# A new order of the work up to the third tile, and low weight parts made in PSUM, in a gated attention and FP4 feed-forward layer

## What is computed

```python
x = x + tanh(g_xattn) * attention(q=layernorm(x), k=v=ctx)        # x 8*512*512, ctx 8*77*512, one head of 512
x = x + tanh(g_ffn) * ffn(layernorm(x))
# attention: softmax((q Wq' + bq)(ctx Wk')' / sqrt(512)) (ctx Wv' + bv) Wo' + bo
# ffn: fp4(silu(fp4(x) fp4(w_gate)') * (fp4(x) fp4(w_up)')) fp4(w_down)'    w_gate, w_up 1408*512, w_down 512*1408
# fp4(x): in blocks of 16 of the last axis, scale = max|x| / 6, x / scale rounded to 0, .5, 1, 1.5, 2, 3, 4, 6, times scale
```

## Time and profile before

| | us |
|---|---|
| median of 3 runs | 951.17 |
| profiled execution, its own time | 951.4 |
| its span on the core | 949.6 |
| TensorE matmul busy | 882.2 (93%) |
| VectorE busy | 760.6 (80%) |
| ScalarE busy | 294.1 (31%) |
| GpSimd busy | 336.9 (35%) |

### The profile page before, as it was taken

One profiled execution on the slowest core, in us unless ns is written; L12 is line 12 of the kernel. 1 busy time (PEld: TensorE's weight loads), 2 busy tenths in 40 slices (PEclk: granted clock), 3 DMA queues, 4 the chain that ended last, 5 costly groups with the idle time before them and its releaser, 6 DMA issues.

```text
span 949.6 us, 11466 instructions
## 1 busy us (share of the span) xinstructions
PE 882.2 (93%) x4233; PEld 457.6 (48%) x4233; DVE 760.6 (80%) x1235; ACT 294.1 (31%) x456; POOL 336.9 (35%) x279
## 2 busy tenths in 40 slices
PE   7959767887599999999999999999999999999996
PEld 4736323543245544554455445545554455444442
DVE  2799977989998879887988798879887988787842
ACT  1444321352223422342234223422342234223220
POOL 1266434424433333333333333333333333333330
PEclk9989878899889999999999999999999999999999
DMA  9512010000533432232223222322222333233222
GB/s 316 213 61 100 14 44 14 12 11 12 131 83 53 98 53 53 53 98 53 53 53 97 53 53 53 98 53 53 54 54 52 53 56 55 51 75 71 53 43 64
DMA packets 141450, 64.62 MB, mean 68 GB/s; under 512 B 126458, under 2 KB 126466, under 8 KB 141393
## 3 DMA queue, kind: packets, MB, share of 16 engines
q1 hardware_dynamic: 141393, 63.88, 28.4%
HBM read 22.76 MB, written 8.39 MB: 33 GB/s over the span
## 4 chain that ended last, share of the span: by engine, by line
PE 73%; DVE 15%; issue 5%; POOL 2%; DMA 2%; SPq 1%; ACT 1%; POOLq 0%; DVEq 0%
PE bank L1226 45%; PE bank L1292 23%; PE bank L1268 3%; DVE arena L844 3%; DVE arena L846 2%; PE bank L1220 2%; DVE wgu_lo L855 1%; POOL arena L428 1%; DMA arena<-in_L_ffn_w_up_dram 1%; DVE xn L905 1%; DVE xwork L801 1%; DMA x_T<-x_parts 1%; DVE h_parts L801 1%; DVE xwork L806 1%; DVE wd L887 0%
## 5 line engine op out<-in xcount | busy, mean ns | idle before, releaser
L1226 PE MATMUL bank<-wgu_hi,x_T 128*128 128x512 f16 (+1 forms) x1536 | 446.2, 365 | 18.1 <-DMA x_T<-x_parts 18.1
L1226 PE MATMUL bank<-wgu_lo,x_T 128*128 128x512 f16 (+1 forms) x768 | 280.4, 365 | 0.0
L1292 PE MATMUL bank<-wd,arena 128*128 128x512 f16 x1056 | 242.4, 387 | 16.9 <-DVE ring L1011 11.5
L1226 PEld LDWEIGHTS bank<-wgu_hi,x_T 128*128 128x128 f16 x1536 | 151.4, 99 | 178.5 <-issue 29.9
L1292 PEld LDWEIGHTS bank<-wd,arena 128*128 128x128 f16 x1056 | 104.7, 100 | 146.4 <-issue 21.7
L428 POOL TENSOR_TENSOR arena<-arena,h_r 128x1024 f32<-128x1024 f32 (+1 forms) x60 | 95.0, 1583 | 139.4 <-DVE h_r L808 139.4
L428 POOL TENSOR_TENSOR arena<-arena,h_s 128x1024 f32<-128x1024 f32 x64 | 89.3, 1395 | 135.0 <-DVE arena L846 135.0
L634 ACT ACTIVATE arena<-bank,scal 128x512 f32<-128x512 f32 (+1 forms) x96 | 62.3, 650 | 193.5 <-PE bank L1226 193.5
L1226 PEld LDWEIGHTS bank<-wgu_lo,x_T 128*128 128x128 f16 x768 | 75.7, 99 | 80.4 <-issue 7.8
L428 POOL TENSOR_TENSOR xwork<-xwork,x_s 128x512 f32<-128x512 f32 x32 | 33.9, 1059 | 185.7 <-DVE xwork L846 185.7
L987 DVE SCALAR_TENSOR_TENSOR arena<-arena,scal,bank 128x512 f32<-128x512 f32 (+1 forms) x90 | 63.0, 700 | 39.9 <-PE bank L1226 39.9
(11 more groups left out here) (117 smaller groups left out, 924.0 us busy)
## 6 DMA issues: line engine op xcount, KB each, us to landing
ring<-in_x_dram SPq DMA_DIRECT2D x8, 1024.0 KB, 5.5
out_dram<-ring SPq DMA_DIRECT2D x32, 256.0 KB, 2.0
arena<-in_L_ffn_w_down_dram SPq DMA_DIRECT2D x4, 704.0 KB, 4.1
arena<-in_L_ffn_w_gate_dram SPq DMA_DIRECT2D x5, 512.0 KB, 11.2
arena<-in_L_ffn_w_up_dram SPq DMA_DIRECT2D x5, 512.0 KB, 11.8
ring<-in_L_xattn_Wk_dram SPq DMA_DIRECT2D x4, 256.0 KB, 4.9
ring<-in_L_xattn_Wq_dram SPq DMA_DIRECT2D x4, 256.0 KB, 5.2
wd<-in_ctx_dram SPq DMA_DIRECT2D x1, 1024.0 KB, 8.8
```

What stands on the lines that cost most here:

```text
L1226: ended = e.matmul(at, l, r, start=(i == 0), stop=(i == len(terms) - 1))
L1292: ended = e.matmul(down_ps[:, :], l, r, start=(k == 0 and i == 0), stop=(k == KH - 1 and i == 2))
```

## The change

Four things, and new lists for all engines up to tile 3 (from `x_stats(4)` on they are as before, but for `h_low(0, 0)` and `h_low(0, 1)`, which now stand ahead of it).

1. The low parts: `gu_fold` multiplies the block scales by the inverse power on ScalarE, so that `gu_times` gives final values; `gu_high` is a plain copy; TensorE adds minus the high part to the bank (one f16 matmul with a negated identity); a ScalarE copy writes the low part. `gu_low` and `down_low` leave VectorE. `gu_times` now waits for the power.
2. The maximum over partitions: transpose of the column of maxima, a reduction on one partition, and a matmul with a row of ones.
3. The keys in two halves (`divmod(i, 5)`): five products before the first scores, five and four value products inside the loop over weight chunks; batch 0's values need `value_product(0)` alone and are read where `value_rows` puts them.
4. Three bf16 buffers for `gu_squares`; loads of weight chunks 0 to 3 between those of `Wk`, `Wq`; `x_turn(0)` ahead of all value moves.

```diff
-            i = WIDE_FROM + j % 2
-            return valo[:, i, :].bitcast(BF16)
+            at = x_parts[:, :] if j % 3 == 0 else x_T[j % 3 - 1][:, :, :].rearrange("p k n -> p (k n)")
...
-        mm = [("bqk", 0)] + [("key", i) for i in range(2 * KD + 2)] + [("vo", m) for m in range(KD)] + [("bvwo", 0)]
-        mm += [("val", r) for r in range(CT)]
+        mm = [("bqk", 0)] + [("key", i) for i in range(KEYS_HALF)] + [("vo", m) for m in range(KD)] + [("bvwo", 0), ("val", 0)]
+        mm += [("key", i) for i in range(KEYS_HALF, 2 * KEYS_HALF)] + [("val", r) for r in range(1, CT)]
         mm_bank = {name: n % 2 for n, name in enumerate(mm)}
-        mm_bank["val", CT - 1] = 5
...
# SyncE
+            for r in range(KD):
+                e.dma_start(stage_a[:, r, :], Wk[r * P:(r + 1) * P, :]).then_inc(loads[f"wk{r}"], 16)
+                e.dma_start(stage_b[:, r, :], Wq[r * P:(r + 1) * P, :]).then_inc(loads[f"wq{r}"], 16)
+                load_gu(r)
...
+            x_turn(0)
+            for n in range(1, NBATCH):
+                move_values(n)
# GpSimd
+            for j in range(EARLY):
+                gu_divide(j)
+            ln1(0)
+            gu_divide(5)
+            gu_times(0)
+            gu_divide(6)
+            gu_times(1)
+            gu_times(2)
+            gu_times(3)
+            gu_divide(7)
...
# ScalarE
-                if j >= 2:
-                    w.wait_ge(gu_neg, j - 1)
+                if j >= 3:
+                    w.wait_ge(gu_neg, j - 2)
...
+            def gu_low(n):
+                w.wait_ge(gu_less, n + 1)
+                e.copy(wgu_lo[:, :, gu_cols(n)], by_k(bank[gu_bank(n)][:, 0:D], KD)).then_inc(gu_lo, 1)
...
+            gu_folds(5, 7)
+            gu_squares(6)
+            for j in range(NPAIR):
...
+                gu_high(2 * j)
+                gu_high(2 * j + 1)
+                if j < 4:
+                    xn_copy(0, j)
+                    vo_copy(j)
...
+                gu_low(2 * j)
+                gu_low(2 * j + 1)
...
+            x_high(0)
+            x_squares(1)
+            x_high(1)
+            down_squares(0)
+            down_squares(1)
+            gate_silu(0, 0)
...
+            gate_silu(1, 2)
+            down_low(1)
+            x_high(3)
+            attention_part(1, "d soft")
+            attention_part(2, "a1")
# VectorE
+            value_rows(2)
+            value_rows(3)
+            x_low(0)
+            x_scales_of(1)
+            x_divide()
+            value_rows(4)
+            down_tops(0)
+            x_round(1)
+            down_tops(1)
+            down_tops(2)
+            x_low(1)
+            down_tops(3)
+            down_top_of()
+            down_scales(0)
+            x_stats(2)
+            power_of(d_top_turned, "d_top", pow_d, d_pow)
+            down_scales(1)
+            hidden(0, 0)
+            down_power()
+            down_scales(2)
+            hidden(0, 1)
+            x_scales_of(2)
+            ln1_stats(1)
+            x_divide()
+            down_round(0)
+            down_scales(3)
+            hidden(0, 2)
+            x_round(2)
+            ln1_apply(1)
...
+            x_low(3)
+            h_scales(0, 0)
+            h_scales(0, 1)
+            hidden(1, 2)
+            softmax(1)
# TensorE
+            def gu_subtract(n):
+                w.wait_ge(negated, 1)
+                w.wait_ge(gu_hi, n + 1)
+                e.matmul(by_k(bank[gu_bank(n)][:, 0:D], KD), neg_ident[:, :], wgu_hi[:, :, gu_cols(n)],
+                         start=False, stop=True, skip_group_check=True).then_inc(gu_less, 1)
...
+            key_product(0)
+            key_product(1)
+            top_turn("gu_top", top_gu, gu_top, gu_top_turned, gu_pow)
+            key_product(2)
+            power_spread("gu_pow", pow_gu, gu_pow, gu_pow_mm, p_ready)
+            key_product(3)
+            key_product(4)
...
+            for j in range(NPAIR):
+                if j == 6:
+                    prob_turn(0)
+                gu_turn(2 * j)
+                gu_turn(2 * j + 1)
+                if 1 <= j < 5:
+                    att_scores(0, j - 1)
+                if j < 4:
+                    att_turn(0, j)
+                    vo_product(j)
...
+                if j == 9:
+                    key_product(9)
+                    value_product(1)
+                if j == 10:
+                    value_product(2)
+                    value_product(3)
+                gu_subtract(2 * j)
+                gu_subtract(2 * j + 1)
+            value_product(4)
+            gate_up(0, 0, 0)
+            top_turn("d_top", top_d, d_top, d_top_turned, d_pow)
+            gate_up(0, 0, 1)
...
+            gate_up(0, 2, 1)
+            attention_part(0, "a3")
+            attention_part(0, "a4")
+            gate_up(1, 0, 0)
...
+            gate_up(1, 2, 0)
+            gate_up(1, 2, 1)
+            down_subtract(1)
+            attention_part(2, "a1")
+            gate_up(2, 0, 0)
```

More of the change, by code:

```diff
@@ new lines, in scalar_program @@
+            w.wait_ge(bqk_mm, 1)
+            e.copy(bqk_col[:, :], bank[mm_bank["bqk", 0]][:, 0:KD]).then_inc(bqk_sb, 1)
+            for r in range(CT):
+                rows = rows_of(r)
+                w.wait_ge(ctx_turned, r + 1)
+                e.copy(ctx_T[:, :, r * P:r * P + rows], by_k(bank[turn_bank["ctx", r]][:, 0:KD * rows], KD)).then_inc(ctx_sb, 1)
+            gu_squares(4)
+            w.wait_ge(loads["ga"], 16)
+            e.activation(tanh_a, tanh_a, ACT.Tanh).then_inc(tanh_done, 1)
@@ new lines, in scalar_program @@
+            w.wait_ge(loads["gf"], 16)
+            e.activation(tanh_f, tanh_f, ACT.Tanh).then_inc(tanh_done, 1)
+            key_copy(0)
+            key_copy(1)
+            key_copy(2)
+            gu_folds(0, EARLY)
+            key_copy(3)
+            gu_squares(5)
+            key_copy(4)
+            for r in range(KD):
+                w.wait_ge(wo_turned, r + 1)
+                e.copy(wo_T[:, :, r * P:(r + 1) * P], by_k(bank[turn_bank["wo", r]][:, 0:D], KD)).then_inc(wo_sb, 1)
+            gu_folds(5, 7)
@@ L757, in scalar_program @@
+            down_low(2)
+            down_high(3)
+            h_squares(0, 1)
+            gate_silu(2, 2)
+            down_low(3)
             h_high(0, 0)
@@ new lines, in vector_program @@
+            gu_tops(1)
+            gu_scales(1)
+            gu_tops(2)
+            gu_scales(2)
+            gu_round(0)
+            gu_tops(3)
+            gu_scales(3)
+            gu_round(1)
+            gu_tops(4)
+            gu_scales(4)
+            gu_tops(5)
+            ln1_stats(0)
+            for j in range(6, NPAIR):
+                gu_tops(j)
+            gu_top_of()
+            gu_scales(5)
+            power_of(gu_top_turned, "gu_top", pow_gu, gu_pow)
+            gu_scales(6)
@@ new lines, in vector_program @@
+            gu_power()
+            ln1_apply(0)
+            gu_round(2)
+            gu_round(3)
+            gu_scales(7)
+            gu_round(4)
+            gu_scales(8)
+            gu_round(5)
+            gu_scales(9)
+            gu_round(6)
+            scale_bo()
+            gu_scales(10)
+            gu_round(7)
+            softmax(0)
+            gu_round(8)
+            sums(0)
+            value_row()
+            value_rows(0)
+            gu_round(9)
+            for i in range(TILES):
+                values(0, i)
@@ new lines, in vector_program @@
+            x_stats(0)
+            gu_round(10)
+            x_scales_of(0)
+            x_divide()
+            value_rows(1)
+            x_round(0)
+            x_stats(1)
+            value_rows(2)
[11 more added lines that the diff above has]
+            down_top_of()
@@ new lines, in vector_program @@
+            x_stats(3)
+            down_round(2)
+            hidden(1, 0)
+            x_scales_of(3)
+            x_divide()
+            down_round(3)
+            hidden(1, 1)
+            x_round(3)
+            x_low(3)
[3 more added lines that the diff above has]
+            softmax(1)
+            sums(1)
+            hidden(2, 0)
+            values(1, 0)
+            h_round(0, 0)
+            hidden(2, 1)
+            values(1, 1)
+            h_round(0, 1)
@@ L1141, in vector_program @@
+            hidden(2, 2)
+            values(1, 2)
+            h_low(0, 0)
+            h_low(0, 1)
             attention_part(3, "a1")
@@ new lines, in tensor_program @@
+            key_product(1)
[4 more added lines that the diff above has]
+            key_product(4)
+            for r in range(KD):
+                take(turn_bank["wo", r], (wo_sb, r + 1))
+                w.wait_ge(loads["wo"], 16)
+                turn(turn_bank["wo", r], [stage_b[:, r, k * P:(k + 1) * P] for k in range(KD)]).then_inc(wo_turned, 1)
@@ new lines, in tensor_program @@
+            for j in range(NPAIR):
+                if j == 6:
+                    prob_turn(0)
[6 more added lines that the diff above has]
+                    vo_product(j)
+                if j == 4:
```

(16 more changed lines are left out.)

638 lines of the change are left out of this document (268 added, 370 removed).

## The result

The changed kernel takes 958.84 us (median of five, 956.52 to 959.73), the one before 951.17 (five runs by now, with the same median); the ratio is 1.0075, 95% interval 1.0052 to 1.0098: slower by 0.75%. 949.5 had been predicted, as no change; what came is the size of the first rival, 960.

A forecast was written before the change was run, and what follows sets the result against it. From tile 4 TensorE never idles, so the time hangs on tile 4's start, and that on when VectorE reaches x_stats(4). 951.4 + 0.4 (x_stats(4) later) - 2.3 (up to tile 4) = 949.5 us; own range 943 to 957.

The forecast's parts named there:

- the first rival: TensorE's two halts in tiles 0 to 2 are longer, x_stats(4) comes at 240: 960 us; chance 0.25.
- The bound: From tile 4 on TensorE never idles; the time is tile 4's start (271.7) plus 677.9 plus 1.8 us.
- Part 1: Setup, the power: scalars ready at 43.0 instead of 46.1, -3; shows only if the next list is short.
- Part 2: Setup, low parts: the 14.5 us removed from VectorE lie in POOL's shadow, worth nothing by themselves.
- Part 3: TensorE's list in the setup: 72.2 us plus waits, ending at 127 (119 to 133); tile 0 at 133, -10.
- Part 4: Tiles 0 to 2, from value_product(3)'s end to x_stats(4): 102.5 us (100 to 112), x_stats(4) at 229.5, +0.4.
- the rule of turns: POOL's product and VectorE's two-input instruction never run together; one with at most one SBUF input doesn't take the pair.
- clock term: Tiles 0 to 2: the clock falls after each halt, the first 12 matmuls taking 4 to 5 us, not 2.6.
- the rule of 28 us: Tiles 0 to 2: the first rival decides as soon as TensorE's two halts together pass 28 us.
- Part 5: From x_stats(4) to tile 4: h_low(0, .) now ahead (1.8), h's transpose no longer waited for (0.5): -2.3 us.
- The sum: Whole kernel: 951.4 + 0.4 - 2.3 = 949.5 us, no measurable change; chance 0.45.
- The other rivals: Setup waits hidden, setup to 120: 940, chance 0.22; all removed VectorE time comes back: 924, chance 0.08.

The follow-up runs named there:

- e7: Changed kernel with the maximum over partitions of the gate and up weights by POOL's partition_all_reduce again, without TensorE's transpose and matmul: 957.92 us, ratio 1.0083.
- e4: Changed kernel with the 22 gate and up low parts back on VectorE, without TensorE's 22 subtractions and ScalarE's 22 copies: 951.73 us, ratio 1.0015.
- e1: Changed kernel with prob_turn(1) moved behind the first three gate_up parts of tile 2: 947.63 us, ratio 0.9966.
- e3: e1 plus gate_silu(0, 0) ahead of down_squares(0) and (1), and the down maxima's transpose behind the second gate_up: 941.29 us, ratio 0.9905.
- e14: Changed kernel with gate_up(0, 2, .) computed twice, on TensorE ahead of its first halt: 957.59 us, ratio 1.0085.
- e10: Changed kernel with batch 1's statistics and rows early and ScalarE's two copies of them directly behind gate_silu(0, 1): 954.00 us, ratio 1.0045.
- e6: e5 with batch 1's statistics and normalized rows moved behind value_rows(3), and a separate buffer for down's first square: 935.34 us, ratio 0.9849.
- e9: e6 with ScalarE's two copies of batch 1's transposed rows directly behind gate_silu(0, 1): 934.52 us, ratio 0.9835.
- e12: e9 with ScalarE's squares of chunks 5 and 6 later, and gate_silu(1, 0) and both copies ahead of down_squares(3): 934.91 us, ratio 0.9833.
- e5: e3 and e4 together, on the changed kernel: 935.29 us, ratio 0.9848.

## Why the prediction was wrong

**The bound, right.** The steady part is unchanged, and the time is the start of tile 4.

**Part 1, right, and worth nothing in the time, as said.** The scalars were ready at 42.4 (43.0 predicted). e7 undoes it alone:

```diff
 # POOL, behind gu_divide(5)
+            e.partition_all_reduce(rest_gu, top_gu, P, bass.bass_isa.ReduceOp.max).then_inc(gu_pow, 1)
 # TensorE
-            top_turn("gu_top", ...)
-            power_spread("gu_pow", ...)
```

> The changed kernel with one part undone: the maximum over partitions of the gate and up weights by POOL's partition_all_reduce again, in front of its first gu_times; no transpose and no matmul on TensorE for it. If the power gates POOL's eleven products and these the setup, then the scalars are ready at 45 instead of 42.3 and all behind is 2 to 3 us later: 961. If TensorE's own list ends the setup, the shift is swallowed by its waits (7.7 for the copies of Wo among them): 958 to 959.

Measured 957.92, against 958.84. ScalarE's first fold of the scales in the changed kernel and in e7:

```profile
42.48 0.56 ACT L599 ACTIVATE valo<-valo,scal 128x320 f32<-128x320 f32 x1 [1.62 <-DVE scal L911]
```

```profile
48.40 0.56 ACT L601 ACTIVATE valo<-valo,scal 128x320 f32<-128x320 f32 x1 [8.63 <-DVE scal L919]
```

The power is 5.9 later, tile 0 begins 1.6 later, and the time is the same. The prediction had the replacement itself at 4 us for the old 4.60 and the rest of its 3 from an earlier last maximum; in e7 the reduction stands behind `gu_divide(5)` and holds VectorE 5.96. TensorE's wait for the copies of Wo, 10.2 for 7.7, took up part of it.

**Part 2, right.** Worth nothing by itself; POOL and VectorE take turns as in the earlier trace rows:

```profile
57.59 1.21 DVE L920 SCALAR_TENSOR_TENSOR arena<-x_T,arena 128x1024 f32<-128x1024 bf16 x1
58.83 2.84 DVE L922 SCALAR_TENSOR_TENSOR arena<-x_T,arena 128x1024 f32<-128x1024 bf16 x1
```

e4 shows that, with what it puts on the other engines, the part costs 5.0 in the setup and 7.1 in the time (5.7 by the ratios), about the 4.8 for subtractions and some of the bank waits in part 3. A slip without effect: 22 x 0.737 is 16.2; the 15.3 is the row's busy time, and the sum went by the pitch, 14.5.

**Part 3, right within 1.4, with a wait in another place.** `value_product(3)` ended at 128.2 (127), the first `gate_up` stood at 134.35 (133), the wait for `value_rows(4)` was there. The wait of 6 had been put in front of the first subtraction, behind `gu_squares(6)`. It was 7.7 and one item earlier: `gu_squares(5)` stands ahead of the copies of Wo and waits 8.25 for VectorE's rounds, so TensorE stood in front of the transposes at 53.59 and made its first subtraction at 61.26 without a wait. That the size came near is luck. The bound of 119 with "no wait" doesn't go with the sum's own 114.8 either.

**Part 4, the step that failed.** The prediction put 102.5 us between the end of `value_product(3)` and `x_stats(4)`; it was 109.5 (237.74 less 128.2). By its own pieces:

| piece | predicted | measured |
|---|---|---|
| up to tile 1's first matmul | 44.5 | 49.3 |
| on to `prob_turn(1)` | 32.2 | 32.8 |
| on to `x_stats(4)` | 25.8 | 27.4 |

So the step that failed is the price of this stretch: POOL's turns and the slow first matmuls behind the halt were put too low, and nothing was put for them ahead of `hidden(0, 0)`. The halts themselves were right, 14.8 for 14 and 9.9 for 9.5, and so was the pause of VectorE (6.17 for 6.2). The first piece holds 4.8 of the 7.0, in three terms. First, `hidden(0, 0)` began 1.0 late: a scaling ahead of it took 1.47, where it takes 0.20 alone. Second, from there to the first normalized row 18.2 us went by instead of 16.7: the work was 14.8 as said, but POOL's turns were taken at 1.9 (range 1 to 6) and were 3.4. Third, from the first transpose behind the halt to tile 1's matmuls it was 4.75 instead of 3.0: TensorE's granted clock is 0.50 there (172.78 to 177.53), its 1.2 GHz level, and a wait of 1.03 for ScalarE's copy lies in it. The last 0.6 are the row itself (172.18 to 172.78). The other pieces add 0.6 and 1.6; what the 1.6 are was not taken apart. The turns are visible in pairs of rows, first VectorE (a scaling of 88 columns, the normalization of x(2), then a reciprocal and another scaling of 88 columns):

```profile
145.36 1.47 DVE L870 TENSOR_SCALAR h_parts<-h_parts 128x88 f32<-128x88 f32 x1
...
157.54 2.05 DVE L1007 TENSOR_SCALAR xwork<-ring,mv,rstd 128x512 f32<-128x512 f32 x1
...
167.84 0.70 DVE L872 RECIPROCAL h_parts<-h_parts 128x88 f32<-128x88 f32 x1
168.58 1.84 DVE L874 TENSOR_SCALAR h_parts<-h_parts 128x88 f32<-128x88 f32 x1
```

then POOL's products:

```profile
144.18 2.59 POOL L450 TENSOR_TENSOR arena<-arena,h_parts 128x1408 f32<-128x1408 f32 x1 [5.90 <-DVE h_parts L874]
...
156.72 2.59 POOL L450 TENSOR_TENSOR arena<-arena,h_parts 128x1408 f32<-128x1408 f32 x1 [5.41 <-DVE h_parts L874]
...
167.77 2.58 POOL L450 TENSOR_TENSOR arena<-arena,h_parts 128x1408 f32<-128x1408 f32 x1 [0.84 <-DVE arena L922]
```

The first scaling ends at 146.83, POOL's product at 146.77. The normalization takes 0.54 where no product holds it up (x(1) at 130.83); here it ends at 159.59, right behind POOL's end at 159.31, and the last scaling at 170.42 behind 170.35. The prediction had the rule of turns from one half only: it said that an instruction with at most one SBUF input is safe. The Trainium skill (SBUF — State Buffer, Who interferes with whom) adds that a `tensor_scalar` can run in a mode that takes the shared pair with one input. The rows agree: all three have one wide input and wait (the scalings take 0.20 alone), while the reciprocal, begun beside the same product, keeps its 0.70. With the turns as they were, 1.0 more ahead of `hidden(0, 0)` and 1.5 more behind it, the same sum gives `x_stats(4)` at 232, not 237.7: the missing half of the rule explains under a third of the miss of 8.2.

The first rival came nearest by number (109 for the stretch, 960), and in part by luck. Its heading is that the two halts are longer, and that it decides once they pass 28 us together; they were 24.7, against 23.5 in the forecast. The first row came at 44.0 (forecast 41.5, rival 46), the setup ended at 128.2 (127 and 131), and its clock term came as said: the first 12 `gate_up` matmuls behind the halt took 4.1 (2.6 and 4 to 5). So the miss is not in longer halts, and the rule of 28 us decided nothing: it is in small terms around halts that were priced rightly. The prediction had written down that the bounds are "open upward only", and still took 102.5, just 2.5 above the lower end of 100 to 112.

**Part 5, right.** -2.3 predicted; from `x_stats(4)` to tile 4 40.0 for 42.6.

**The sum.** 949.5 and the miss of `x_stats(4)`, 8.2 (1.2 from part 3, 7.0 from part 4), is 957.7; the profiled execution was 957.4.

**The other rivals.** The setup was not hidden (134.35, not 120), and the removed time of VectorE did not come back (e4).

**What the loss is made of.** The setup gave 8.8, part 5 gave 2.6, and the stretch took 17.4. Of the 17.4, e1 to e3 returned 16.4 by order alone. So the loss isn't in the operations but in where a few short items stand: `prob_turn(1)` ahead of tile 2 (10.6) and the SiLU behind two squares (3.5). The other 2.3 are a difference: e3 also moved the maximum's transpose, which no run moved alone. The first halt of 14.8, the longest wait in the profile, is not among them: 4.1 us of work put into it cost nothing (e14), and what e10 gained, 4.9, came with 4.4 us less of VectorE's work in the stretch.

**What stays open.** With the order mended the stretch is 83 to 87, and three ways to shorten TensorE's first halt (e6, e9, e12) took 3.4 from it at most. The rows of e12 point to a row through `x_squares(3)`, `down_low(0)`, `down_turn(1)`, `down_subtract(1)` and `x_high(3)` with pauses on VectorE, ScalarE and TensorE in turn; no run cut it. Nor was it tried to put the low parts of down back on VectorE.

## What to carry to other kernels

A long wait of an engine need not be a cost: the longest here was free, because the engine that sets the end was busy meanwhile. Compare the busy and the idle time of both over the stretch (here VectorE 73.8 and 72.6 busy, 12 and 31 idle) and price the pauses of the one that counts, not the halts of the other. That names the place and not yet the cure: in e12 the pause stayed when the halt in front of it was cut. In orders written by hand look for a short item that needs a long chain and stands ahead of work that needs nothing: one such item cost 10 to 11 us of 950. Where two engines take turns, ask of time taken from one whether it lay beside the other's work: here giving 14 us back to VectorE, and the matmuls and copies in their place up, made the kernel some 6 us faster (e4, e5).
